# A graph-attention layer on one core: g and p's scale straight from d, a third bank for h, and new instruction orders up to the end of the first group

## The reference

```python
h = jnp.maximum(_layernorm(x, axis=-1), 0.0)
h = h @ W.T                                   # 256 x 256
src = h @ a1
dst = h @ a2
e = leaky_relu(src[:, None] + dst[None, :], negative_slope=0.2)
e = where(adj == 0, -9e15, e)
attention = softmax(e, axis=1)
out = x + attention @ h
```

## Time and profile before

| | us |
|---|---|
| median of 3 runs | 384.66 |
| lowest, highest | 383.90, 385.73 |
| the profiled execution's own time | 384.0 |
| its span, first to last instruction | 382.4 |

### The profile page before, as it was taken

The page is one execution under the profiler, slowest core; times in us unless marked ns, Lnnn a source line. Parts: engine busy times, 40 slices in busy tenths (PEclk is TensorE's granted clock), DMA queues, the critical chain, the costliest instruction groups (busy, mean ns, idle before and its releaser), DMA issues.

```text
span 382.4 us, 9231 instructions
## 1 busy us (share of the span) xinstructions
PE 376.6 (98%) x3358; PEld 330.5 (86%) x3358; DVE 362.8 (95%) x456; ACT 195.7 (51%) x272; POOL 43.1 (11%) x68
## 2 busy tenths in 40 slices
PE   8999899999999999999999999999999999999996
PEld 6788688888888888888888888888888888888885
DVE  4999999999999999999999999999987999999965
ACT  5999754744443644344445543444446443444430
POOL 3897020000000001110000002100000011100001
PEclk9999999999999999999999999999999999999999
DMA  7931476857676666776666667766665567666503
GB/s 252 374 78 42 136 228 223 278 165 233 221 222 215 210 218 221 235 231 224 220 218 205 216 209 234 239 222 222 216 208 184 169 216 244 232 219 225 171 2 111
DMA packets 27025, 78.23 MB, mean 205 GB/s; under 512 B 3956, under 2 KB 9336, under 8 KB 27000
## 3 DMA queue, kind: packets, MB, share of 16 engines
q1 hardware_dynamic: 25568, 74.59, 60.4%
q0 software_dynamic: 1280, 3.16, 2.2%
q10 hardware_dynamic: 152, 0.13, 0.1%
HBM read 73.66 MB, written 4.21 MB: 204 GB/s over the span
## 4 chain that ended last, share of the span: by engine, by line
PE 96%; ACT 1%; DMA 1%; issue 1%; DVE 0%; ACTq 0%
PE ps L1435 88%; PE ps L1259 2%; PE ps L1274 2%; PE ps L1285 2%; PE ps L1280 2%; DMA a_rows<-a 1%; PE ps L1224 1%; PE ps L1240 1%; ACT c_row L517 0%; ACT h_sb L491 0%; DVE rows_sb L1153 0%; ACT L643 0%; ACT p_hi L527 0%; ACTq L502 0%; PE ps L1234 0%
## 5 line engine op out<-in xcount | busy, mean ns | idle before, releaser
L1435 PE MATMUL ps<-v_sb,p_hi 128*128 (+2 forms) x2048 | 251.9, 273 | 1.0 <-ACT p_hi L527 0.9
L537 ACT ACTIVATE p_hi<-p_sb,gp 128x1024 f16<-128x1024 f32 x126 | 144.4, 1149 | 166.5 <-DVE p_sb L816 140.0
L1435 PEld LDWEIGHTS ps<-v_sb,p_hi 128*128 128x128 f16 x2048 | 199.6, 98 | 26.9 <-issue 1.2
L823 DVE SCALAR_TENSOR_TENSOR p_lo<-p_sb,gp,p_hi 128x1024 f16<-128x1024 f32 x126 | 160.7, 1277 | 7.2 <-ACT p_hi L537 6.7
L816 DVE SCALAR_TENSOR_TENSOR p_sb<-c_row,gp,adj_sb 128x1024 f32<-128x1024 uint32 (+1 forms) x126 | 160.5, 1278 | 0.0
L1435 PE MATMUL ps<-v_sb,p_lo 128*128 (+1 forms) x1024 | 141.6, 273 | 0.0
L1435 PEld LDWEIGHTS ps<-v_sb,p_lo 128*128 128x128 f16 x1024 | 100.0, 98 | 12.8 <-DVE p_lo L823 0.2
L467 POOL DMA_DIRECT2D out<-rows_sb x24 | 13.0, 541 | 263.0 <-DVE rows_sb L1117 262.9
L416 POOL TENSOR_SCALAR hn_sb<-x_sb,moments,rstd 128x256 f32<-128x256 f32 x17 | 21.3, 1260 | 4.1 <-DVE rstd L765 3.2
L775 DVE SCALAR_TENSOR_TENSOR hnt_lo<-ps,hnt_hi 128x256 f16<-128x256 f32 x32 | 12.9, 410 | 0.3 <-ACT hnt_hi L507 0.2
L1274 PE MATMUL ps<-w_hi,hnt_hi 128*128 128x258 f16 x64 | 12.5, 277 | 0.4 <-ACT h_sb L491 0.4
(11 more groups left out here) (87 smaller groups left out, 87.9 us busy)
## 6 DMA issues: line engine op xcount, KB each, us to landing
adj_sb<-adj_t SPq DMA_DIRECT2D x128, 512.0 KB, 4.8
x_sb<-x SPq DMA_DIRECT2D x7, 512.0 KB, 8.5
out<-rows_sb POOLq DMA_DIRECT2D x24, 128.0 KB, 4.6
c_row<-c_flat SPq DMA_DIRECT2D x3, 512.0 KB, 6.7
out<-rows_sb SPq DMA_DIRECT2D x7, 128.0 KB, 1.8
x_sb<-x SPq DMA_DIRECT2D x2, 256.0 KB, 3.5
c_row<-s_flat SPq DMA_DIRECT2D x1, 512.0 KB, 3.9
w_nat<-w SPq DMA_DIRECT2D x1, 256.0 KB, 2.8
```

What stands on the lines that cost most here:

```text
L537: nc.scalar.activation(p_hi[:, u % R, :], p_sb[:, u % R, :], ACT.Copy, scale=p_scale[:, bass.ds(t, 1)])\
L823: nc.vector.scalar_tensor_tensor(out=p_lo[:, u % R, :], in0=p_sb[:, u % R, :], scalar=p_scale[:, bass.ds(t, 1)], in1=p_hi[:, u % R, :], op ...
L1435: return nc.tensor.matmul(ps[:, k, 0:width], part[:, u % R, k * P:(k + 1) * P], v_sb[:, bass.ds(t, 1), v, 0:width], start=start, stop=stop ...
```

## The change

What it does, part by part:

- **Normalisation.** Tile 0 goes from ScalarE to GpSimd; in all ScalarE has 10 tiles (14 before), GpSimd 19 (17), VectorE 3 (1).
- **Values.** GpSimd casts the pairs from 0, 2, 10 and 26 (before 0, 4, 8, 10, 12), ScalarE the other twelve; the casts stand elsewhere in the orders.
- **Banks.** h goes through three banks (6, 7, 4), so a tile waits for the tile three before it; d's spread goes to bank 5, d's turn to bank 2, with a wait for the low part of the last tile that was turned there.
- **g and p's scale.** gp_args and exp_gp are gone. ScalarE takes both exponentials straight from d's column of h, with a scale and a bias of its own for each; VectorE makes p_bias, GpSimd one more scale.
- **Orders.** TensorE's projections of several tiles interleave, and tile 0's first sums stand ahead of tile 31's last projections. w_hi and w_lo come in halves at other places. The transposition of c moves from before split_lo(4) to behind split_lo(10). The orders of value_hi, value_lo, edge_weights and split_lo in the first group are new. What each engine does in the later groups is as before.

The diff, cut to its core:

```diff
-    BY_VECTOR = [26]
-    BY_SCALAR = [0, 1] + list(range(4, 14, 2)) + [15, 19, 21, 23, 24, 25, 29]
-    BY_GPSIMD = [2] + list(range(3, 15, 2)) + [14, 16, 17, 18, 20, 22, 27, 28, 30, 31]
+    BY_VECTOR = [24, 25, 27]
+    BY_SCALAR = [1, 4, 7, 8, 10, 12, 14, 15, 18, 20]
+    BY_GPSIMD = [0, 2, 3, 5, 6, 9, 11, 13, 16, 17, 19, 21, 22, 23, 26, 28, 29, 30, 31]
-    HIGH_BY_SCALAR = [2, 6] + list(range(14, T, 2))
-    HIGH_BY_GPSIMD = [0, 4, 8, 10, 12]
+    HIGH_BY_SCALAR = [4, 6, 8, 12, 14, 16, 18, 20, 22, 24, 28, 30]
+    HIGH_BY_GPSIMD = [0, 2, 10, 26]
...
-        bank_w, bank_n, bank_d, bank_e = 4, 1, 4, 5
-        bank_h = 6
+        bank_w, bank_n, bank_d, bank_e = 4, 1, 5, 2
+        banks_h = (6, 7, 4)
+        HB = len(banks_h)
...
+            def exp_g(t0, t1):
+                act.wait_ge(c_bias_ready, 1)
+                act.wait_ge(h_kept, t1)
+                nc.scalar.activation(g_col[:, t0:t1], h_sb[:, t0:t1, F + 1], ACT.Exp,
+                                     bias=exp_bias[:, 0:1], scale=exp_scale[:, 1:2]).then_inc(g_ready, 1)
+
+            def exp_p(t0, t1):
+                act.wait_ge(p_bias_ready, 1)
+                act.wait_ge(h_kept, t1)
+                nc.scalar.activation(p_scale[:, t0:t1], h_sb[:, t0:t1, F + 1], ACT.Exp,
+                                     bias=p_bias[:, 0:1], scale=exp_scale[:, 3:4]).then_inc(p_scale_ready, 1)
...
             keep_h(28)
+            exp_g(0, R)
             exp_c(0)
+            exp_c(1)
+            exp_p(0, R)
+            exp_c(2)
+            exp_c(3)
+            hi_part(0, 0)
             keep_h(29)
-            exp_gp(slice(0, R), 1)
-            exp_c(1)
-            exp_c(2)
-            hi_part(0, 0)
-            exp_c(3)
             hi_part(0, 1)
...
             nc.vector.reciprocal(w_scale[:], norms[:]).then_inc(w_scale_ready, 1)
-            rstd_of(0)
             dve.wait_ge(w_scale_ready, 1)
             nc.vector.scalar_tensor_tensor(out=wa_scale[:], in0=w_scale[:, 0:1], scalar=1 / W_UP, in1=w_scale[:, 1:2],
                                            op0=ALU.mult, op1=ALU.mult).then_inc(wa_scale_ready, 1)
+            rstd_of(0)
             shift_of(0)
...
+            split_w_lo(0)
...
+            rstd_of(1)
+            stats_of(4)
+            stats_of(5)
             stats_of(6)
             gather(4)
             stats_of(7)
             gather(5)
             gather(6)
             gather(7)
+            split_w_lo(1)
+            split_hn_lo(0)
...
             nc.vector.tensor_scalar(exp_bias[:], d_safe[:], exp_scale[:, 2:3], None, ALU.mult).then_inc(c_bias_ready, 1)
             dve.wait_ge(c_bias_ready, 1)
-            nc.vector.tensor_scalar(gp_args[:, 0, 0:R], h_sb[:, 0:R, F + 1], exp_scale[:, 1:2],
-                                    exp_bias[:, 0:1], ALU.mult, ALU.add).then_inc(g_args_ready, 1)
-            dve.wait_ge(g_args_ready, 1)
-            nc.vector.tensor_scalar(gp_args[:, 1, 0:R], gp_args[:, 0, 0:R], 0.25, math.log(P_UP), ALU.mult, ALU.add)\
-                .then_inc(gp_args_ready, 1)
+            nc.vector.tensor_scalar(p_bias[:], exp_bias[:], 0.25, math.log(P_UP), ALU.mult, ALU.add).then_inc(p_bias_ready, 1)
+            split_hn_lo(31)
             value_lo(10)
...
             split_lo(2, 10, 8)
+            dve.wait_ge(c_col_ready, 1)
+            nc.vector.transpose(c_blocks[:], c_col[:]).then_inc(c_blocks_ready, 1)
             dve.wait_ge(p_lo_ready, 9)
             edge_weights(4, 12, 64, 0)
...
             edge_weights(6, 30, 128, 0)
             split_lo(5, 29, 24)
+            split_lo(6, 30, 24)
+            shift_of(6)
             dve.wait_ge(p_lo_ready, 28)
             edge_weights(7, 31, 128, 0)
-            split_lo(6, 30, 24)
             split_lo(7, 31, 24)
...
             spread_d()
+            project_hi(28)
+            project_hi(29)
+            turn_d()
+            project_w_lo(28)
+            project_hi(30)
+            project_lo(28)
...
+            project_hi(31)
+            high_sums(0, 0)
+            project_w_lo(31)
+            project_lo(31)
+            high_sums(0, 1)
```

More of the change, by code:

```diff
@@ new lines, in _ @@
+            turn(0)
+            turn(1)
+            turn(2)
+            project_hi(0)
+            project_hi(1)
+            project_w_lo(0)
+            project_hi(2)
+            project_w_lo(1)
+            turn(3)
+            project_lo(0)
+            project_lo(1)
+            project_w_lo(2)
+            turn(4)
+            turn(5)
+            project_lo(2)
+            project_hi(3)
+            project_w_lo(3)
+            project_hi(4)
+            project_w_lo(4)
+            turn(6)
@@ new lines, in _ @@
+            turn(7)
+            project_lo(3)
+            project_lo(4)
+            project_hi(5)
+            project_w_lo(5)
+            project_lo(5)
+            project_hi(6)
+            project_w_lo(6)
+            project_lo(6)
+            turn(8)
+            project_hi(7)
+            project_w_lo(7)
+            turn(9)
+            turn(10)
+            project_lo(7)
+            project_hi(8)
+            turn(11)
+            project_hi(9)
+            project_w_lo(8)
+            project_lo(8)
@@ new lines, in _ @@
+            project_w_lo(9)
+            project_hi(10)
+            project_w_lo(10)
+            project_lo(9)
+            project_hi(11)
+            project_w_lo(11)
+            turn(12)
+            turn(13)
+            project_lo(10)
+            project_lo(11)
+            turn(14)
+            project_hi(12)
+            project_w_lo(12)
+            project_lo(12)
+            turn(15)
+            project_hi(13)
+            turn(16)
+            project_w_lo(13)
+            project_hi(14)
@@ new lines, in _ @@
+            turn(17)
+            project_lo(13)
+            project_hi(15)
+            project_w_lo(14)
+            project_w_lo(15)
+            project_lo(14)
+            project_lo(15)
+            project_hi(16)
+            project_w_lo(16)
+            turn(18)
+            project_lo(16)
+            turn(19)
+            project_hi(17)
+            project_w_lo(17)
+            turn(20)
+            project_hi(18)
+            project_w_lo(18)
+            turn(21)
+            project_lo(17)
@@ new lines, in _ @@
+            project_lo(18)
+            project_hi(19)
+            turn(22)
+            project_w_lo(19)
+            project_hi(20)
+            project_w_lo(20)
+            project_lo(19)
+            turn(23)
+            project_lo(20)
+            project_hi(21)
+            project_w_lo(21)
+            turn(24)
+            project_lo(21)
+            project_hi(22)
+            project_w_lo(22)
+            turn(25)
+            turn(26)
+            project_hi(23)
+            project_lo(22)
@@ new lines, in _ @@
+            project_w_lo(23)
+            project_hi(24)
+            turn(27)
+            project_w_lo(24)
+            turn(28)
+            project_lo(23)
+            project_hi(25)
+            project_lo(24)
+            turn(29)
+            project_w_lo(25)
+            project_lo(25)
+            turn(30)
+            project_hi(26)
+            project_w_lo(26)
+            project_lo(26)
+            turn(31)
+            project_hi(27)
+            project_w_lo(27)
+            project_lo(27)
```

545 lines of the change are left out of this document (207 added, 338 removed).

## The result

The changed kernel takes 384.90 us (median of 22 runs, 384.31 to 386.42), the kernel before 384.18 on the same chip (22 runs, 383.68 to 385.73). The ratio is 1.002, with a 95% interval of 1.0013 to 1.0027: +0.72 us, slower, and by less than the 0.5% that counts as a change. The profiled execution took 384.6 us, 0.6 more than the one of before, and its span is 382.9 against 382.4.

The account below looks back on a forecast made before the run. TensorE, busy 98%, bounds the kernel, with VectorE close behind and 0.3 us of cover at the first group's end. Group end +0.3 and late load +0.3 make +0.6 us on 384.0, median 385.3; range 383.0 to 387.2.

Parts of the forecast that it names:

- the stretching: GpSimd's last five normalisations in the opening: slowed beside VectorE's work by 0.65 us in all, ends 0 and 1.7.
- the transposition: c's later transposition delays SP's loads; edge load of tile 16 comes 0.3 us late, ends 0 and 2.6.
- The start: Opening's first 23 matmul pairs on TensorE: out at about 14.25 instead of 14.96, 0.7 us won.
- The middle: Opening up to tile 31's turn, released by GpSimd: turn(31) at 34.4, bounds 33.8 to 35.5, against 34.97.
- Rival (c): End of the opening: GpSimd's last tiles stretch three times, turn(31) at 35.5; 386.4 us, chance 0.10.
- (e): Opening: GpSimd and TensorE reach turn(31) as late as before, so the start gains nothing; 386.1 us, chance 0.07.
- To the first sums: From turn(31) on: exp_bias 0.57 us earlier at 37.4, TensorE idle about 2.2, first full split 0.8 earlier.
- The early gain: From the opening to VectorE's first full split and TensorE's tile 3: 0.8 us gained, bounds -0.3 and 1.6.
- The end of the first group: Split 30 ahead of edge 31: VectorE idles 1.3 us before split 31, TensorE's tile 31 +0.3, bounds 0 and 1.4.
- Rival (a): First group's end: VectorE runs far enough ahead that its wait isn't seen; 383.3 to 383.9 us, chance 0.20.
- (d): Opening runs gapless, turn(31) at 33.3, and VectorE's later wait isn't seen; 382.6 us, chance 0.06.
- Rival (b): SP's queue: loads behind c_flat's stores make tile 16's edges 2.6 us late; 387.6 us, chance 0.12.

Follow-up runs that it names:

- E11: Kernel before with only the three banks for h and d's turned copies in other banks: 383.85 us, ratio 1.0001.
- E10: Kernel before with only g and p's scale made by two exp straight from d, no gp_args: 384.09 us, ratio 1.0003.
- E1: Changed kernel with split 30 put back behind edge 31: 383.76 us, ratio 1.0005; 383.22 us at full clock.
- E5: Changed kernel with split 30 back behind edge 31 and five filler matmuls ahead of the first sums: 383.16 us, ratio 0.998.
- E2: Kernel before with only split 30 moved ahead of edge 31: 385.16 us, ratio 1.0031.
- E3: Changed kernel with c's transposition early again, behind split 4: 384.70 us, ratio 1.0028; 384.45 us at full clock.
- E9: E5 with c's transposition early again, at the place the kernel before had it: 383.36 us, ratio 0.9984.
- E8: Kernel before with eight unread copies on ScalarE ahead of its first hi_part, to add idle time on TensorE: 385.92 us, ratio 1.0052.
- E7: Changed kernel with only five filler matmuls added ahead of the first sums: 384.56 us, ratio 1.0019.
- E12: E5 with tile 0 normalised by ScalarE again instead of GpSimd: 383.68 us, ratio 1.0008.
- E6: Changed kernel with split 30 back behind edge 31, first hi_part right behind exp_p and three filler matmuls: 383.59 us, ratio 0.9995.

## Why the prediction was right, step by step

The forecast was +0.6 us on the profiled execution and 385.3 for the median; it came to +0.6 and 384.90. The 385.3 stood on 384.66, the median of three runs of the kernel before; 22 runs of it give 384.18, and against these the change is +0.72. The steps that carried the forecast stand, two terms do not (the stretching and the transposition), and one effect was missing. That the sum fits to a tenth is partly luck: in the middle, and in what the transposition's 0.3 us stood for.

- **The start:** 14.25 predicted, 14.29 in the profile. This is closer than the step deserves: over the nine profiled executions with the changed opening, turn(31) lies anywhere from 33.68 to 34.60. And GpSimd's early tile 0, the first of its reasons, carries little of it. Of TensorE's 23 pairs the first five are out at 10.41 before and 10.29 after, 0.12 us apart, and the other 18 take 4.55 us before and 4.00 after, 0.222 each, without a gap. First before:

```profile
10.41 0.38 PE L1274 MATMUL ps<-w_hi,hnt_hi 128*128 128x258 f16 x2
...
14.96 0.38 PE L1274 MATMUL ps<-w_hi,hnt_hi 128*128 128x258 f16 x2
```

Then after (the row of 14.29 is above):

```profile
10.29 0.38 PE L1286 MATMUL ps<-w_lo,hnt_hi 128*128 128x258 f16 x2
```

So 0.55 of the 0.67 us come where the projections interleave, the step's other reason. The third bank alone does not bring it (E11).

- **The middle:** turn(31) at 34.4 predicted, 34.38 found, but by terms that made up for each other. GpSimd's last five normalisations, beside three of VectorE's and the value_lo, took 6.25 us (row below), 5 x 1.21 = 6.05 without stretching: 0.2, where I had 0.65. They began 0.3 later than I had walked (33.8 - 6.05 = 27.75), 0.21 of it a wait for rstd(6).

```profile
28.08 6.25 POOL L418 TENSOR_SCALAR hn_sb<-x_sb,moments,rstd 128x256 f32<-128x256 f32 x5 [0.21 <-DVE rstd L777]
```

It was VectorE that was held once: 0.59 instead of 0.42 us, in its row of 28.18 above. The three full blocks of 0.42 us that the Trainium skill's page "SBUF — State Buffer" would give ("Who interferes with whom") would have put turn(31) at 35.0; the trace shows none. Rival (c), three stretched normalisations, falls with that, and (e) with the 0.6 us that turn(31) came earlier. The five profiled executions with the opening of before have turn(31) at 34.63 to 35.02, all later than the nine.

- **To the first sums:** exp_bias 37.37 (37.4 predicted), the first full split 46.59 (46.7). The idle time ahead of the sums is 2.52 (2.2): ScalarE's first hi_part starts 2.80 us after exp_bias, where I had 2.46. That the removed gp_args give VectorE nothing holds: its first weights start 1.25 us after exp_bias (38.62), 1.31 before, as the moved split takes their place. E10 adds a second reason, as there no split moves and ScalarE becomes the one waited for.
- **The early gain:** 0.8 predicted; E1 shows 0.72 at full clock and E5 0.78, at the end of the run, where nothing else spends it.
- **The end of the first group:** 1.3 us of VectorE idle, TensorE's tile 31 0.3 later: 1.22 and 0.38 measured. Split 31 starts 2.50 us behind edge 31 (119.97 to 122.47), as I had summed it. Rival (a), that this wait would not be seen, falls with TensorE's own wait there (0.86 us in its row, where I had named over 1) and with E1 and E2; (d) needed (a) and falls with it.
- **The transposition of c:** the term of +0.3 us was mis-sized. c_flat landed when I said (load at 73.1, 73.3 predicted), but adj 16 was not late: its loads landed 4.8 us after 73.47, at 78.3, as VectorE came to it. Undone, it gives a gain of 0.15 us at full clock in E3 and a loss of 0.2 in E9: nothing that can be told from zero. Rival (b) falls. The sum came out right because what I had there came from elsewhere: 0.14 us behind the first group in the profile, and in the median the clock.
- **What was missing: the clock.** I named TensorE's idle time of some 2 us ahead of the first sums and costed it as a wait alone. In 9 of 22 runs of the changed kernel it also took the clock down for a while, which raises the median by 384.90 - 384.60 = 0.3 us. Such an execution loses 1.6 us in E1 and 0.6 here, where, as I read it, the wait at the group's end takes the rest.

## What to carry to other kernels

When two engines hand a tile back and forth, an instruction that stands between a producer and the wait for its consumer is cover; look at what stands behind it before moving it forward for its own sake. Gaps gathered into one are not the same as the same gaps spread out: one long idle time of TensorE can cost its clock, in some executions only, so look at each run's granted clock when a kernel begins to scatter, and fill the gap. A single profile compares two versions only from the point up to which they agree.

## What the runs showed that I had not expected

- The clock falls in some executions and not in others: in 21 of 44 with the same idle time, 2.52 us. And it falls after TensorE has begun to work again (E8: idle to 42.16, full clock up to 43, half from 44).
- 1.4 us left behind fillers never brought it down (0 of 45 in E5, E7, E9 and E12), while E11's 1.39 without fillers did in 2 of 11. What tells these apart was not tried.
- The opening scatters by 0.9 us from execution to execution with nearly the same order of instructions, up to turn(31). The scatter is there early: the first project_w_lo starts anywhere from 9.68 to 10.53 us in the nine profiles, and in eight of them turn(31) follows it by 23.99 to 24.09 us (E6: 24.32). What sets it was not tried.
